# Two unrolled loops and a reordered state space layer in a six-layer kernel on one Trainium2 core

## The chip, the cores and the metric

The kernel runs on one core of one Trainium2 chip, in one launch. The metric is device time in microseconds (us). The core has five engines that run their own instruction queues and meet at semaphores: TensorE (PE, with PEld for its weight loads), VectorE (DVE), ScalarE (ACT), GpSimd (POOL) and SyncE (SP), which issues most of the DMA transfers.

## The reference

Six layers, each added to the residual `x` (128 sequences of 32 tokens, 256 channels), all behind a layer norm:

```python
x = x + L0_xattn(ln(x), ctx, ctx, mask)   # softmax cross-attention, 16 heads of 16, 257 context rows
x = x + L0_attn(ln(x))                    # state space layer, 16 states for each channel
x = x + L0_ffn(ln(x))                     # quantised feed-forward layer
x = x + L1_xattn(ln(x), ctx, ctx)         # the same attention with a sigmoid in place of the softmax
x = x + L1_attn(ln(x))                    # self-attention with a bias
x = x + L1_ffn(ln(x))                     # 8 experts, one for each token
```

The state space layer, cut to what matters:

```python
xc, z = split(x @ W_in.T)
xs = silu(conv3(xc))                       # over neighbouring tokens
dt = softplus(dt_param @ W_dt.T + b_dt) + 1e-5
s  = exp(-exp(A_log) * dt) * s + Bp * dt * xs          # scan over the 32 tokens
y  = (Cp @ W_C.T) * s.sum(-1) + D_param * xs
out = (y @ W_out.T) * silu(z)
```

## The kernel before

The residual stays in the on-chip memory (`all_xres`) through all layers. The layers run one after another, called x0 (softmax attention), m0 (state space), f0, x1 (sigmoid attention), a1 and e1; between two of them all engines meet. Matrix products are made from fp16 pairs (`...h` and `...l`, high and low part), three products for each.

**x0 and x1.** The unit of work is one sequence (128 of them). For each, PE makes the keys (`x_psK`) and values (`x_psV`) from the context, then the scores (`x_psS`: line 548 in x0, line 1190 in x1) and the attention sums; x0 also transposes the probabilities. ACT and DVE split each result into a high and a low part, POOL splits the context and spreads the queries. Four sequences make a group, which shares a tile of queries; eight sequences, two groups, make one body, so a layer is 16 bodies. Each engine has its own function `body(i)`, in which the order is written by hand: scores of sequence c, keys of c+2, transposes of c-1, values of c+1, attention of c-2 on PE, and so on. Where a body has an index that is a Python number, all its addresses and semaphore values are constants; where it is a loop's register, they are worked out at run time. The helper `run` (lines 251 to 255 in x0, 981 to 985 in x1) writes out body 0 and body 15 and puts the 14 between them in a hardware loop:

```python
def run(eng, body):
    body(0)
    with eng.Fori(1, LASTI) as i:
        body(i)
    body(LASTI)
```

In x0 the last context row is handled apart. `last_scores` (its products are recorded under line 432, as `x_psM<-x_kxh,x_qbdh`) runs once for each group, 24 products of two columns each, and takes its keys at an address that depends on the group.

**m0.** The unit is a tile of 256 tokens, 16 of them, four to a body; bodies 1 and 2 are in a hardware loop (line 1671). For a tile n, PE does `drive` (line 1852, products that fill `m_psBx`, four quarters), `state_sum` (line 1863, the sum over states, four pieces of eight), and for neighbouring tiles `xc` and `z` (input projections), `dbl` (the projection to dt, B and C parameters), `dt_c` (dt and C), `uT` (line 1839, a transpose of `m_u`), `xnT` and `out`. DVE scans each quarter (line 2077) and does the convolution, the low parts, `read_out` and `gate` (line 2091). ACT does the 32 exponentials of `decay` (line 1984), the logarithm `softplus_log` (line 1964), the two silu functions (lines 1930 and 1937) and high parts. POOL does `split_xs` (lines 1700 and 1702), `dt_u` (lines 1715 and 1718: dt, then u = dt times xs), `spread_b` (line 1725), `read_out` and `residual` (line 1743). `m_psBx` has one buffer: a quarter's drive waits for the scan of the quarter before it. The order on each engine is the order of the calls in `body`.

Of the kernel before, what the change touches and what calls it, by code (L numbers as in the profile page):

```python
# [180 lines left out]
def softmax_attention(nc, d, xres, con, norm):  # L181
# [4 lines left out]
    with ExitStack() as ctx:  # L186
# [62 lines left out]
        LASTI = NT // 2 - 1  # L249

        def run(eng, body):
            body(0)
            with eng.Fori(1, LASTI) as i:
                body(i)
            body(LASTI)

        def exists(i, c, off):
            return not isinstance(i, int) or 0 <= i * 8 + c + off < NB
# [664 lines left out]
def sigmoid_attention(nc, d, xres, con, norm):  # L923
# [4 lines left out]
    with ExitStack() as ctx:  # L928
# [50 lines left out]
        LASTI = NT // 2 - 1  # L979

        def run(eng, body):
            body(0)
            with eng.Fori(1, LASTI) as i:
                body(i)
            body(LASTI)

        def exists(i, c, off):
            return not isinstance(i, int) or 0 <= i * 8 + c + off < NB
# [627 lines left out]
def state_space(nc, d, xres, con, norm):  # L1616
# [7 lines left out]
    with ExitStack() as ctx:  # L1624
# [65 lines left out]
        @block.gpsimd  # L1690
        def _(pool):
            pool.memset(up[:], UP).then_inc(zeroed, 1)
            for h in range(C):
                pool.memset(A[h][:], 0.0).then_inc(zeroed, 1)

            def split_xs(i, c):
                n = i * U + c
                wait_apart(pool, xs_done, n + 1, pool_passed)
                wait_apart(pool, pb_mm, n, pool_passed)
                pool.tensor_scalar(xsp[0][:], xs[c % 2][:], 1.0, 1.0, ALU.mult, ALU.mult).then_inc(xs_hi, 1)  # L1700
                pool.wait_ge(xs_hi, n + 1)
                pool.tensor_tensor(xsp[1][:], xs[c % 2][:], xsp[0][:], ALU.subtract).then_inc(xs_lo, 1)

            def direct(i, c):
                n = i * U + c
                wait_apart(pool, y_done, n - 3, pool_passed)
                for h in range(C):
                    last = pool.tensor_scalar(dxs[c][:, h, :], xs[c % 2][:, h, :], d_par[:, h:h + 1], YS, ALU.mult, ALU.mult)
                last.then_inc(dxs_done, 1)

            def dt_u(i, c):
                n = i * U + c
                pool.wait_ge(soft_step, n * 4 + 4)
                wait(pool, a_done, (n - 1) * C)
                pool.tensor_tensor(dt[c % 2][:], sp_r[:], sp_a[:], ALU.add).then_inc(dt_done, 1)
                pool.wait_ge(dt_done, n + 1)
                wait(pool, u_mm, n - 1)
                pool.tensor_tensor(u[c % 2][:], dt[c % 2][:], xs[c % 2][:], ALU.mult).then_inc(u_done, 1)

            def spread_b(i, c):  # L1720
                n = i * U + c
                pool.wait_ge(pb_lo, n + 1)
                wait(pool, bx_mm, (n - 1) * 4)
                for k in range(2):
                    last = pool.tensor_tensor(Bd[c % 2][k][:], Bp[k][:].unsqueeze(2).to_broadcast([P, 2 * NS, T]),
                                              token[:].unsqueeze(1).to_broadcast([P, 2 * NS, T]), ALU.mult)
                last.then_inc(b_spread, 1)

            def read_out(i, c):
                n = i * U + c  # L1730
                pool.wait_ge(y_prod, n + 1)
                pool.tensor_tensor(y[:], y[:], dxs[c][:], ALU.add).then_inc(y_done, 1)
                wait_apart(pool, y_done, n + 1, pool_passed)
                wait_apart(pool, o_mm, n, pool_passed)
                pool.tensor_scalar(yp[0][:], y[:], 1.0, 1.0, ALU.mult, ALU.mult).then_inc(y_hi, 1)
                pool.wait_ge(y_hi, n + 1)
                pool.tensor_tensor(yp[1][:], y[:], yp[0][:], ALU.subtract).then_inc(y_lo, 1)

            def residual(i, c):
                n = i * U + c  # L1740
                pool.wait_ge(o_done, n + 1)
                row = xres[:, bass.ds(n * (2 * D), 2 * D)]
                pool.tensor_tensor(row, row, o[:], ALU.add).then_inc(x_done, 1)

            pool.wait_ge(const_in, 80)
            for c in range(2):
                split_xs(0, c)
                direct(0, c)
                if c == 0:
                    dt_u(0, 0)  # L1750
                    spread_b(0, 0)

            def body(i):
                for c in range(U):
                    if exists(i, c, 1):
                        spread_b(*at(i, c, 1))
                    if exists(i, c, -2):
                        residual(*at(i, c, -2))
                    if exists(i, c, 1):
                        dt_u(*at(i, c, 1))  # L1760
                    if exists(i, c, 2):
                        split_xs(*at(i, c, 2))
                    if exists(i, c, -1):
                        read_out(*at(i, c, -1))
                    if exists(i, c, 2):
                        direct(*at(i, c, 2))
            run(pool, body)
            residual(LASTI, U - 2)
            read_out(LASTI, U - 1)
            residual(LASTI, U - 1)  # L1770

        @block.tensor
        def _(pe):
# [111 lines left out]
            def body(i):  # L1885
                for c in range(U):
                    drive(i, c, 0)
                    if exists(i, c, 2):
                        xc(*at(i, c, 2))
                        z(*at(i, c, 2))  # L1890
                    if exists(i, c, -1):
                        state_sum(*at(i, c, -1), 1, 0)
                    drive(i, c, 1)
                    if exists(i, c, -1):
                        state_sum(*at(i, c, -1), 1, 1)
                    if exists(i, c, 1):
                        uT(*at(i, c, 1))
                    if exists(i, c, 3):
                        xnT(*at(i, c, 3))
                    drive(i, c, 2)  # L1900
                    state_sum(i, c, 0, 0)
                    if exists(i, c, -1):
                        out(*at(i, c, -1))
                    if exists(i, c, 2):
                        dbl(*at(i, c, 2))
                    drive(i, c, 3)
                    state_sum(i, c, 0, 1)
                    if exists(i, c, 2):
                        dt_c(*at(i, c, 2))
            run(pe, body)  # L1910
            state_sum(LASTI, U - 1, 1, 0)
            state_sum(LASTI, U - 1, 1, 1)
# [3 lines left out]
        def _(act):  # L1916
# [83 lines left out]

            def body(i):
                for c in range(U):
                    decay(i, c, 1, 0)
                    decay(i, c, 1, 1)
                    if exists(i, c, 1):
                        softplus_log(*at(i, c, 1))
                    if exists(i, c, 2):
                        silu_z(*at(i, c, 2))
                        silu_xs(*at(i, c, 2))
# [16 lines left out]
        def _(dve):  # L2026
# [75 lines left out]
            def body(i):  # L2102
                for c in range(U):
# [10 lines left out]
                    scan(i, c, 2)  # L2114
                    if exists(i, c, 2):
                        lo_pb(*at(i, c, 2))
                    scan(i, c, 3)
                    if exists(i, c, -1):
                        gate(*at(i, c, -1))
                    if exists(i, c, 4):  # L2120
                        ln(*at(i, c, 4))
            run(dve, body)
# [1076 lines left out]
```

## Time and profile before

| what | value |
|---|---|
| three timed runs | 3118.89, 3127.29, 3130.5 us (median 3127.29) |
| the profiled execution, its own time | 3123.87 us |
| its span in the trace | 3122.1 us |
| PE busy | 2561.8 us, 82% |
| DVE busy | 2130.9 us, 68% |
| ACT busy | 1878.5 us, 60% |
| POOL busy | 1542.9 us, 49% |
| mean granted TensorE clock | 0.913 of full speed |
| x0, from its first scores to its last | 56.6 to 940.5 us |
| m0, between the first and the last transposes and products of PE | 980 to 1475 us |
| x1, from its first scores to its last | 1660.6 to 2313.6 us |

How to read it: the engines work side by side, so their busy times do not add up to the span. A share over the whole span mixes six layers that have different limits; what a change in one layer is worth has to be read from that layer's own stretch. An idle time is given with what ended it: a tile of another engine, or "issue", where nothing that the profile shows was waited for.

### The profile page before, as it was taken

The page shows a single profiled execution, that of the slowest core. Times are in us where ns is not written, and L with a number is a line of the kernel's source. Part 1 is how long each engine was busy: PE and PEld are TensorE (multiplying, and loading weights), DVE is VectorE, ACT ScalarE, POOL GpSimd, SP SyncE. Part 2 cuts the span into 40 slices and gives each one's busy share as a digit, 9 for nine tenths or more (in the row PEclk, how much of TensorE's full clock was granted, in tenths as well). Part 3 has the DMA queues.
Part 4 walks back from the last instruction along what each step waited for, and adds up shares of the span by engine and source line. Part 5 has one row for each costly group of instructions (what it writes and reads, how often), then busy time and mean ns, then how long its engine had stood idle before and what let it go on. Part 6 is the DMA issues. An engine that isn't in the chain of part 4 may idle for free. (4 is left out here: it accounts for less than half of the span.)

```text
span 3122.1 us, 105389 instructions
## 1 busy us (share of the span) xinstructions
PE 2561.8 (82%) x38670; PEld 2034.0 (65%) x38671; DVE 2130.9 (68%) x4719; ACT 1878.5 (60%) x4388; POOL 1542.9 (49%) x1680
## 2 busy tenths in 40 slices
PE   3989889899893899996778989989967878509888
PEld 2867777677782577774446868768755666507666
DVE  5978878788794788886355757657665887643333
ACT  3867667677684788883346767667654665333333
POOL 4655656556562355552006656656635776052222
PEclk9999999999996899998898999999987998559999
DMA  4212212112110000000003212112100000641110
GB/s 144 67 59 59 64 51 64 58 51 64 57 30 14 1 1 1 0 1 14 16 14 91 66 50 62 59 52 61 59 18 3 2 2 2 206 159 34 33 34 27
DMA packets 120602, 144.45 MB, mean 46 GB/s; under 512 B 12912, under 2 KB 111632, under 8 KB 118064
## 3 DMA queue, kind: packets, MB, share of 16 engines
q1 hardware_dynamic: 115568, 124.40, 13.2%
q0 software_dynamic: 4672, 14.57, 1.3%
q8 instruction: 307, 5.03, 0.7%
q14 instruction: 55, 0.45, 0.0%
HBM read 123.71 MB, written 15.22 MB: 44 GB/s over the span
## 5 line engine op out<-in xcount | busy, mean ns | idle before, releaser
L1368 DVE SCALAR_TENSOR_TENSOR x_pTl<-x_psS,x_pTh 128x1024 f16<-128x1024 f32 x128 | 156.8, 1225 | 206.8 <-ACT x_pTh L1276 206.8
L2077 DVE TENSOR_TENSOR_SCAN m_s<-m_a,m_psBx 128x2048 f32<-128x2048 f32 x64 | 282.6, 4415 | 16.0 <-PE m_psBx L1852 15.6
L791 DVE CUSTOM_DVE_ANT_0 x_prob<-x_psS,x_masked,x_prob 128x256 f32<-128x256 f32 x512 | 216.6, 478 | 73.5 <-PE x_psS L548 71.7
L664 ACT ACTIVATE x_prob<-x_prob,x_low 128x257 f32<-128x257 f32 x512 | 253.5, 503 | 20.6 <-DVE x_low L791 20.6
L680 ACT ACTIVATE x_kh<-x_psK,x_bk 128x256 f16<-128x256 f32 x256 | 107.5, 471 | 238.9 <-PE x_psK L432 238.9
L1863 PE MATMUL m_psS<-m_s,all_ident 128*128 128x256 f32 x1024 | 237.3, 385 | 0.9 <-DVE m_s L2077 0.9
L1863 PEld LDWEIGHTS m_psS<-m_s,all_ident 128*128 128x128 f32 x1024 | 190.0, 190 | 46.3 <-issue 21.5
L1984 ACT ACTIVATE m_a<-m_dt,m_rate 128x248 f32<-128x248 f32 x512 | 205.6, 490 | 4.3 <-DVE m_s L2077 4.1
L2982 ACT ACTIVATE e1t_g<-e1t_psH,e1t_bias 128x128 f32<-128x128 f32 x312 | 89.2, 368 | 194.5 <-PE e1t_psH L2931 194.5
L1057 POOL TENSOR_TENSOR x_qbdh<-x_qh,all_mask4h 128x1024 f16<-128x1024 f16 x32 | 60.6, 1895 | 226.7 <-DVE x_ql L1349 226.7
L806 DVE SCALAR_TENSOR_TENSOR x_pTl<-x_psT,x_pTh 128x512 f16<-128x512 f32 x256 | 163.5, 679 | 4.9 <-ACT x_pTh L672 4.0
L1270 ACT ACTIVATE x_psS<-x_psS 128x1024 f32<-128x1024 f32 x128 | 129.0, 1008 | 59.7 <-PE x_psS L1190 57.3
L1049 POOL TENSOR_TENSOR x_ctxl<-x_ctx,x_ctxh 128x512 f16<-128x512 f32 x128 | 149.5, 1168 | 10.7
L337 POOL TENSOR_TENSOR x_ctxl<-x_ctx,x_ctxh 128x512 f16<-128x512 f32 x128 | 148.9, 1163 | 10.7
L432 PE MATMUL x_psK<-x_ctxh,x_wkh 128*128 128x256 f16 x512 | 148.3, 290 | 5.8 <-POOL x_ctxl L337 3.4
L2931 PE MATMUL e1t_psH<-e1t_xnh,e_wh 128*128 128x128 f16 x624 | 144.6, 232 | 9.0 <-issue 8.5
L1096 PE MATMUL x_psK<-x_ctxh,x_wkh 128*128 128x256 f16 x512 | 144.3, 282 | 4.5 <-POOL x_ctxl L1049 3.0
L432 PE MATMUL x_psK<-x_ctxh,x_wkl 128*128 128x256 f16 x512 | 147.8, 289 | 0.0
L432 PE MATMUL x_psK<-x_ctxl,x_wkh 128*128 128x256 f16 x512 | 147.8, 289 | 0.0
L1289 ACT ACTIVATE x_vh<-x_psV 128x512 f16<-128x512 f32 x128 | 76.4, 597 | 118.3 <-PE x_psV L1096 118.3
L672 ACT ACTIVATE x_pTh<-x_psT 128x512 f16<-128x512 f32 x256 | 138.9, 594 | 12.0 <-PE x_psT L558 9.2
L1096 PE MATMUL x_psK<-x_ctxl,x_wkh 128*128 128x256 f16 x512 | 143.3, 280 | 0.0
(558 smaller groups left out, 10542.0 us busy)
## 6 DMA issues: line engine op xcount, KB each, us to landing
x_ctx<-in_ctxT SPq DMA_DIRECT2D x64, 1024.0 KB, 5.7
x_mraw<-in_mask SPq DMA_DIRECT2D x128, 128.5 KB, 2.7
e1r_stage<-in_L_ffn_w SPq DMA_DIRECT2D x16, 1024.0 KB, 5.0
e_rows<-e1r_pad POOLq DMA_DIRECT2D x1, 5070.0 KB, 19.5
e1t_row<-e_rows SPq DMA_DIRECT2D x39, 130.0 KB, 2.1
all_xres<-in_x SPq DMA_DIRECT2D x1, 4096.0 KB, 14.8
x_vxr<-x_vx SPq DMA_DIRECT2D x128, 32.0 KB, 3.2
x_vxr<-x_vx SPq DMA_DIRECT2D x96, 8.0 KB, 2.0
```

Source lines behind the costliest of these rows:

```text
L337: pool.tensor_tensor(lo[:, j], src, hi[:, j], ALU.subtract).then_inc(ctx_split, 1)
L432: last = pe.matmul(out, a, b, start=m == 0, stop=m == len(prods) - 1)
L664: act.activation(prob[c % 4][:, h, :], prob[c % 4][:, h, :], ACT.Exp, bias=low[c % 4][:, h:h + 1], scale=-1.0, accum_out=sm[c % 2][:, h:h ...
L791: dve.tensor_tensor_reduce(prob[c % 4][:, h, 0:LAST], psS[:, to:to + LAST], masked[gp][:, j, 0:LAST], -SC, prob[c % 4][:, h, LAST:S2], ALU ...
L806: dve.scalar_tensor_tensor(pT[c % 2][1][:, kt, :], psT[:, kt * 512:(kt + 1) * 512], PS, pT[c % 2][0][:, kt, :], ALU.mult, ALU.subtract).th ...
L1049: pool.tensor_tensor(lo[:, j], src, hi[:, j], ALU.subtract).then_inc(ctx_split, 1)
L1096: last = pe.matmul(out, a, b, start=m == 0, stop=m == len(prods) - 1)
L1368: dve.scalar_tensor_tensor(pT[c % 4][1][:].rearrange("p r k n -> p (r k n)"), psS[c % 2][:], PS, pT[c % 4][0][:].rearrange("p r k n -> p ( ...
L1863: last = pe.matmul(psS[:, h * ST:(h + 1) * ST], con["ident"][:], S[h][:, :, m, :], start=m == 0, stop=m == NS - 1)
L1984: last = act.activation(A[h][:, :, m, 1:T], dt[c % 2][:, h, :].rearrange("p (b t) -> p b t", t=T)[:, :, 1:T], ACT.Exp, scale=rate[:, h, m: ...
L2077: dve.tensor_tensor_scan(rows(S), rows(A), psBx[:], 0.0, ALU.mult, ALU.add).then_inc(scan_done, 1)
L2931: last = pe.matmul(bank[:, k % 4 * P:(k % 4 + 1) * P], a, b, start=m == 0, stop=m == len(prods) - 1)
```

## The change

Three parts. In x0 and x1 `run` no longer makes a hardware loop: all 16 bodies are written out, on all five engines, with constants for every address and semaphore value. In m0, which keeps its loop, six calls change their place in the queues of POOL, PE, ACT and DVE. No operation is added or removed by hand.

```diff
@@ x0 (line 251) and, with the same text, x1 (line 981)
         def run(eng, body):
-            body(0)
-            with eng.Fori(1, LASTI) as i:
+            for i in range(LASTI + 1):
                 body(i)
-            body(LASTI)
@@ m0, POOL
                         spread_b(*at(i, c, 1))
+                        dt_u(*at(i, c, 1))
                     if exists(i, c, -2):
                         residual(*at(i, c, -2))
-                    if exists(i, c, 1):
-                        dt_u(*at(i, c, 1))
@@ m0, PE
                     state_sum(i, c, 0, 0)
+                    if exists(i, c, 2):
+                        dbl(*at(i, c, 2))
                     if exists(i, c, -1):
                         out(*at(i, c, -1))
-                    if exists(i, c, 2):
-                        dbl(*at(i, c, 2))
                     drive(i, c, 3)
-                    state_sum(i, c, 0, 1)
                     if exists(i, c, 2):
                         dt_c(*at(i, c, 2))
+                    state_sum(i, c, 0, 1)
@@ m0, ACT
+                    if exists(i, c, 1):
+                        softplus_log(*at(i, c, 1))
                     decay(i, c, 1, 0)
                     decay(i, c, 1, 1)
-                    if exists(i, c, 1):
-                        softplus_log(*at(i, c, 1))
@@ m0, DVE
-                    scan(i, c, 3)
                     if exists(i, c, -1):
                         gate(*at(i, c, -1))
+                    scan(i, c, 3)
```

The first place is PE in x0, in a body between the first and the last, where `last_scores` begins (`x_kxh` and `x_kxl` are the keys of the last context row, `x_qbdh` the queries). Before:

```order
L472 MATMUL x_psM<-all_ident,x_px 96x128
L476 ISA
L432 ISA
L432 MATMUL x_psM<-x_kxh,x_qbdh 128x2
L432 REGISTER_ALU
L432 MATMUL x_psM<-x_kxl,x_qbdh 128x2
L432 MATMUL x_psM<-x_kxh,x_qbdl 128x2
L432 ISA
```

Now (the file is five lines shorter here and there, so line numbers differ by two to five):

```order
L556 MATMUL x_psT<-all_ident,x_prob 128x128 x8
L470 MATMUL x_psM<-all_ident,x_px 96x128
L430 MATMUL x_psM<-x_kxh,x_qbdh 128x2
L430 MATMUL x_psM<-x_kxl,x_qbdh 128x2
L430 MATMUL x_psM<-x_kxh,x_qbdl 128x2
```

The register instructions between the products (`ISA` and `REGISTER_ALU`, one of each to every three products, eight times) are gone, and with them those at the waits of every body and the branch at its end.

The second place is PE in m0, the second half of a tile. Before (`m_psC<-m_xsh` is `dbl`, `m_psZ<-m_wouth` is `out`, `m_psC<-m_pbh` and `m_psU<-m_pbh` are `dt_c`, L1863 is `state_sum`):

```order
L1863 MATMUL m_psS<-m_s,all_ident 128x256 x8
L1777 MATMUL m_psZ<-m_wouth,m_yh 128x256
...
L1777 MATMUL m_psC<-m_xsh,m_wxh 96x256
...
L1852 MATMUL m_psBx<-m_bd1h,m_ut1l 128x512 x4
L1863 MATMUL m_psS<-m_s,all_ident 128x256 x8
L1777 MATMUL m_psC<-m_pbh,m_wdch 128x256
...
L1777 MATMUL m_psU<-m_pbh,m_wdch 128x256
```

Now:

```order
L1858 MATMUL m_psS<-m_s,all_ident 128x256 x8
L1772 MATMUL m_psC<-m_xsh,m_wxh 96x256
...
L1772 MATMUL m_psZ<-m_wouth,m_yh 128x256
...
L1847 MATMUL m_psBx<-m_bd1h,m_ut1l 128x512 x4
L1772 MATMUL m_psC<-m_pbh,m_wdch 128x256
...
L1772 MATMUL m_psU<-m_pbh,m_wdch 128x256
...
L1858 MATMUL m_psS<-m_s,all_ident 128x256 x8
```

`dbl` has moved ahead of `out`, and `dt_c` ahead of the last piece of the state sum.

The third place is ACT in m0, from the end of one tile to the middle of the next. Before:

```order
L1959 ACTIVATE m_sp_a<-m_sp_a 128x512
L1970 ACTIVATE m_c<-m_psU 128x512
L1984 ACTIVATE m_a<-m_dt,m_rate 128x8x31 x16
L1964 ACT_TABLE_LOAD
L1964 ACTIVATE m_sp_a<-m_sp_a,m_up 128x512
L1930 ACT_TABLE_LOAD
L1930 ACTIVATE m_zs<-m_psZ 128x512
```

Now:

```order
L1954 ACTIVATE m_sp_a<-m_sp_a 128x512
L1965 ACTIVATE m_c<-m_psU 128x512
L1959 ACT_TABLE_LOAD
L1959 ACTIVATE m_sp_a<-m_sp_a,m_up 128x512
L1979 ACT_TABLE_LOAD
L1979 ACTIVATE m_a<-m_dt,m_rate 128x8x31 x16
L1925 ACT_TABLE_LOAD
L1925 ACTIVATE m_zs<-m_psZ 128x512
```

The logarithm has moved ahead of the sixteen exponentials, and one more table load stands in each tile: the table is changed for the logarithm and changed back for the exponentials.

## Rows read from the trace of the kernel before

**Rows 1.** The page, part 1: busy us (share of the span) xinstructions

```profile
PE 2561.8 (82%) x38670; PEld 2034.0 (65%) x38671; DVE 2130.9 (68%) x4719; ACT 1878.5 (60%) x4388; POOL 1542.9 (49%) x1680
```

**Rows 2.** Windows, x0: stretch, length, busy PE PEld DVE ACT POOL, PEclk, DMA, GB/s

```profile
82.50:106.14 23.64, 23.09 (x458) 19.54 (x456) 21.74 (x69) 20.56 (x66) 14.53 (x23) 1.00 0.14 38
106.14:161.33 55.19, 48.92 (x911) 40.83 (x910) 48.05 (x148) 40.19 (x125) 39.45 (x61) 0.98 0.26 80
161.33:218.48 57.15, 50.74 (x908) 41.96 (x909) 46.10 (x142) 39.44 (x122) 33.77 (x50) 0.95 0.20 59
...
901.82:925.33 23.51, 22.89 (x456) 19.21 (x454) 21.07 (x67) 19.50 (x62) 16.16 (x25) 1.00 0.01 4
```

**Rows 3.** Waits in 106:902, PE and DVE: us in total, times, longest

```profile
PE x_psS L548 <- issue: 69.0, 13, 5.5
PE x_psS L548 <- DVE x_low L791: 10.5, 27, 0.5
...
DVE x_ql L765 <- ACT x_px L656: 28.2, 28, 1.3
...
DVE x_prob L791 <- issue: 0.3, 1, 0.3
```

**Rows 4.** Timeline of PE in x0: start, us, engine, line, operation, out<-in, [idle before]

```profile
97.46 0.17 PE L432 MATMUL x_psM<-x_kxh,x_qbdh 128*128 128x2 f16 x1
...
98.06 0.27 PE L432 MATMUL x_psV<-x_wvh,x_ctxh 128*128 128x256 f16 x1
...
106.14 0.28 PE L548 MATMUL x_psS<-x_kh,x_qbdh 64*128 64x256 f16 x2
...
146.01 0.17 PE L432 MATMUL x_psM<-x_kxh,x_qbdh 128*128 x1
...
147.95 0.27 PE L432 MATMUL x_psV<-x_wvh,x_ctxh 128*128 128x256 f16 x1
...
161.33 0.39 PE L548 MATMUL x_psS<-x_kh,x_qbdh 64*128 64x256 f16 x2 [5.36 <-issue]
...
901.82 0.28 PE L548 MATMUL x_psS<-x_kh,x_qbdh 64*128 64x256 f16 x2
```

**Rows 5.** Windows of x1, columns as in rows 2

```profile
1678.66:1697.82 19.16, 19.16 (x417) 15.65 (x417) 13.68 (x23) 14.42 (x23) 15.32 (x14) 1.00 0.33 97
...
1819.08:1865.80 46.72, 40.97 (x833) 32.89 (x834) 27.66 (x44) 28.95 (x46) 25.79 (x22) 0.90 0.18 54
```

**Rows 6.** Waits of the whole run for L1190, then the timeline of PE in x1

```profile
PE x_psS L1190 <- issue: 34.1, 6, 5.7
...
1697.82 0.23 PE L1190 MATMUL x_psS<-x_qbdh,x_kh 64*128 64x128 f16 x2
...
2282.23 0.23 PE L1190 MATMUL x_psS<-x_qbdh,x_kh 64*128 64x128 f16 x2
```

**Rows 7.** DMA queues in 56.6:161, 161.33:901.82, 1736.31:1810: packets, MB, share

```profile
q8 instruction: 15, 0.25, 1.0%
q14 instruction: 9, 0.07, 0.2%
...
q8 instruction: 116, 1.90, 1.1%
...
q14 instruction: 1, 0.01, 0.0%
```

**Rows 8.** m0: windows (columns as in rows 2), then the waits in 1060:1381

```profile
1060.00:1167.00 107.00, 99.98 (x747) 76.73 (x746) 93.72 (x73) 90.32 (x193) 54.59 (x48) 1.00 0.00 1
...
PE m_psU L1839 <- POOL m_u L1718: 18.2, 12, 1.6
```

**Rows 9.** Timeline of ACT and PE in one tile of m0

```profile
1172.68 1.28 ACT L1964 ACT_TABLE_LOAD   x1
1173.97 0.72 ACT L1964 ACTIVATE m_sp_a<-m_sp_a,m_up 128x512 f32<-128x512 f32 x1
...
1177.52 0.33 PE L1839 MATMUL m_psU<-all_ident,m_u 128*128 128x128 f32 x1 [1.57 <-POOL m_u L1718]
```

More of the change, by code:

```diff
@@ L981, in run @@
         def run(eng, body):
-            body(0)
-            with eng.Fori(1, LASTI) as i:
+            for i in range(LASTI + 1):
                 body(i)
-            body(LASTI)
         def exists(i, c, off):
```

## The prediction

> **What bounds the kernel now.** I read the page first: PE is the busiest engine, 82% of the span, DVE 68%, ACT 60% [rows 1]. That is a mean over six layers, so I went to the windows of the three layers that the change touches, then to the waits, then to the timeline where the waits said "issue".
>
> x0, between its bodies 1 and 14, is bound by PE with one hole per body. A body in the hardware loop lasts 57.15 us, in which PE is busy 50.74 and DVE 46.10 [rows 2]. Over the whole loop PE sat idle before the scores 13 times until "issue", 69.0 us in total, and 27 times on DVE for 10.5 us [rows 3]. The timeline shows where: 5.36 us before the first scores of body 2, at 161.33, but nothing at 106.14, where body 1 follows the written-out body 0, nor at 901.82, where body 15 follows the loop [rows 4]. Thirteen holes for 14 passes of the loop: they stand at the backward branch. The reader should also see the clock. It is 1.00 in the stretches without a hole and 0.95 in a body that begins after one [rows 2]; 1.00 is the 2.4 GHz level throughout, and 0.95 is a mean with a piece at 1.2 GHz in it, after PE had stood idle for 5.36 us.
>
> x1 shows the same, less often: 6 holes in 13 backward branches, 34.1 us [rows 6]. A body behind a hole has 40.97 us of PE work at a clock of 0.90, while a written-out half body lasts 19.16 us and is filled by PE to the last hundredth, at 1.00 [rows 5].
>
> m0 is nearly full on PE: 99.98 of 107.00 us (four tiles), DVE 93.72, ACT 90.32 [rows 8]. Most of PE's idle time there has one cause: the transpose of u waits for POOL, 18.2 us in 12 tiles, up to 1.6 us each [rows 8], and POOL waits for the logarithm on ACT, which stands behind sixteen exponentials.
>
> **The sum.** All of it is against the profiled execution, 3123.87 us for a span of 3122.1, which lies 3.4 us under the median of 3127.29.
>
> x0. The 14 bodies of the loop run from 106.14 to 901.82 [rows 4]: 795.7 us, or 56.83 each. The written-out code gives its own price in this trace. The second half of body 0, with every step of a full half body in it, lasts 23.64 us, and the first half of body 15, which lacks one layer norm and its transposes, 23.51 [rows 2]. I take 23.64: 28 halves make 661.9, so the gain is 133.8 us. Three things make it up. The holes are 69.0 [rows 3]. The register instructions between the 24 small products of `last_scores` stretch them from 97.46 to 98.06 (0.60 us) to 146.01 to 147.95 (1.94 us) [rows 4]: 1.34 us, 28 times, 37.5 us. What is left, 27 us, is about 2.1 us for each hole, the products that ran at the low clock behind it and the DVE work that came late. The ends of the gain: if the `last_scores` part does not come through, a body is body 1 without its hole, 55.19 - 5.36 = 49.83 [rows 2, 4], and the gain 98. If half bodies take 23.51, it is 137.
>
> Does DVE let PE run at 23.64? It is busy 46.10 in a body [rows 2], 23.05 in a half, and waits 2.0 us a body for ACT in `lo_q` (28.2 us in the whole loop, 28 times) [rows 3], which hangs on ACT's own queue and does not go with the holes. 23.05 + 1.0 makes 24.1 for a half, over 23.64. But in the half that I take the price from DVE did the same instructions. I keep 23.64 and give the difference to a rival.
>
> x1. The loop runs from 1697.82 to 2282.23 [rows 6], 584.4 us; 28 halves at 19.16 [rows 5] are 536.5. The gain is 47.9, of which 34.1 are holes [rows 6] and the rest the low clock behind them. The bounds are close, since seven bodies of the loop run at about 38.5 already: 42 to 49.
>
> Instruction fetch. The written-out bodies have to be read from memory as they run. For PE that is nothing new in x0: the instruction queue q8 brought 116 pages of 16 KB in 161.33 to 901.82, nine for each body, in the loop too, and 15 in the first two bodies [rows 7], where PE never waited for "issue" by 1 us. In x1 it is new, since the loop ran for whole bodies without a packet in q8 (1736.31 to 1810 shows q14 alone) [rows 7]; but the half body at 1678.66 ran from fresh pages and is full [rows 5]. The other engines' queue q14 brought 9 small pages in 56.6 to 161 and none in the loop [rows 7]. I cost all of it at nothing; the cover is that pages arrive ahead while the engine works on the last one, and DVE's longest wait for "issue" in x0 is 0.3 us [rows 3]. The Trainium skill, page "Runtime: NRT & Kernel Launch", section "Instruction fetch mechanics", says that prefetch runs straight ahead and that a taken branch whose target is outside a window of two pages has to fetch before it can go on. By that every backward branch of x1 would stall, 13 times, and the gain there would be about 13 x 7.6 = 99 us. The trace has 6 of 13 [rows 6], and loop and written-out half are both measured; they decide, and I stay at 47.9.
>
> m0. PE has 99.98 / 4 = 25.0 us of work in a tile of 26.75 [rows 8]. The reorder can give no more than the difference, 1.75. I expect it to give nearly that. The logarithm comes 16 exponentials sooner, so u is there before PE asks (1.57 us idle at 1177.52 [rows 9]). With `dbl` ahead of `out` and `dt_c` ahead of the last state sum, ACT gets both of its inputs earlier, and stands less between them and the next tile's softplus. What is paid: ACT gets one more table load in each tile, 1.28 us [rows 9], 90.32 / 4 + 1.28 = 23.9 us, still under 25.0, so PE hides it; `hi_u` now queues behind the silu functions, which the saved wait for u covers; `dt_c` may wait a few tenths for `lo_pb` on DVE; POOL's `residual` waits 1.3 us later behind `dt_u`, and nobody waits for it within the tile. Over 14 full tiles I take 14 x 1.75 = 24.5. The bounds: 0 if another wait takes the place, and a loss of 16 x 1.28 = 20 if ACT's load lands on the path. I take the gain because the three waits that the edits shorten are all on PE's side, and PE is the nearest to full. The Trainium skill, page "ScalarE: Activation LUTs", section "Table sets: the hidden batching unit", says that exponential and logarithm share one set, so that the moved logarithm would need no load at all. Here the logarithm has its own load of 1.28 us right ahead of it [rows 9]. By the page ACT would need 22.6 - 1.3 = 21.3 us a tile, before and after, and the sum would stay as it is, since PE ends the tile. The same page's section "What ACT_TABLE_LOAD costs" puts a switch at about 2.66 us with its drain; by that ACT would need 25.3 us a tile and m0 would gain about 4 us less.
>
> Sum: 133.8 + 47.9 + 24.5 = 206.2; 3123.9 - 206.2 = 2917.7, say **2918 us**. Other layers keep their code. Their loops may lose or gain a hole of some 5 us, since their pages lie elsewhere now.
>
> **Rivals.** *DVE becomes the bound of x0.* At 24.1 to 24.9 a half the gain is 121 down to 98 and the time 2930 to 2954. For it: the 2.0 us of waits a body [rows 3] and a busy share that is already 46.10 of 47.3. Against it: both written-out halves [rows 2].
>
> *m0 gives nothing or loses.* The table load and the silu functions behind the exponentials delay xs and u for the next tile; the time is 2942 with no gain, 2962 with a loss of 20. For it: ACT would be busy 95% of a 25 us tile. Against it: 1.1 us of slack.
>
> *The change doesn't do what it says.* The holes of x0 could belong to every ninth page and not to the branch, since there are nine pages to a body [rows 7]. Then written-out code keeps them, x1 stays as it is, and only `last_scores` and m0 gain: 3124 - 37.5 - 24.5 = 3062. Against it: 15 pages in the first two bodies without a hole, and 9 pages in x0 against none in x1 for much the same hole.
>
> *Slower than before.* The pages of DVE, ACT, POOL and SP, which the loops never reread, stall their engine. At 4.5 pages a body in x0 and about 2 in x1, that is some 90 pages; a stall of 5.4 us each, passed on to PE, costs 490 us, and the time is 3124 - 206 + 490 = 3408. It decides from 2.3 us a page. For it: in x0 DVE has half a microsecond of slack in a half body, so every stall would show. Against it: 0.3 us as the longest of DVE [rows 3] with 9 such pages read.
>
> **How the numbers follow.** Forecast 0.62; DVE-bound x0 0.18; m0 without gain 0.12; holes that stay 0.04; slower 0.03; no change at all, by some mixture, 0.01. The likeliest gives 2918. The low end is the upper bounds together (137 + 49 + 25 = 211) less the 5 us by which the timed runs lie under the profiled one: 2908, taken to 2902 for m0 edges. The high end takes in m0 without gain (2942) and nearly all of a DVE-bound x0 (2954), one at a time: 2950, which leaves out the losing m0, the holes that stay and the slower case, some 0.15 in all. A measurement of this kernel can tell about 0.5% (16 us) from no change. Faster by more: 0.96; within: 0.01; slower: 0.03.
>
> **What would show it.** In x0 no wait of PE for "issue" over 1 us before the scores, steps of 47.3 us from body to body, a clock of 1.00, and `last_scores` in 0.6 us each. In x1 steps of 38.3 us, PE full. In m0 tiles of about 25.0 us, no wait of PE for POOL's u, four table loads a tile. I am wrong if holes of 2 us or more appear anywhere in the written-out code, if DVE's wait for ACT in `lo_q` grows and PE waits for DVE's scores more than 0.5 us a half, or if m0's tile stays at 26.75.

## The result and the profile after

The changed kernel took 2898.18 us, median of 4 runs (2896.4 to 2903.61), against 3124.8 us for the kernel before on the same chip (4 runs, 3118.89 to 3130.5): a ratio of 0.9278 with a 95% interval of 0.9255 to 0.9301. The prediction was 2918 us with a range of 2902 to 2950. The direction and most of the size are right, but the time lies 4 us under the range: the prediction was wrong, and the last sections say by which step. The profiled execution took 2897.14 us, its span is 2895.3 us.

Part 1 of the page of the changed kernel, which answers to [rows 1]:

```profile
PE 2477.0 (86%) x38670; PEld 1973.2 (68%) x38671; DVE 2113.1 (73%) x4719; ACT 1896.3 (65%) x4402; POOL 1537.3 (53%) x1680
```

PE has the same 38670 products and is busy 84.8 us less, 66.3 of them in x0 and 13.7 in x1. I read this as the part of the gain that was low clock, or register instructions between products. ACT has 14 instructions more, the table loads of m0.

Windows of the changed kernel, columns as in [rows 2]: the second half of x0's body 0, bodies 1, 2, and the whole stretch of the former loop; then one body of x1 and its former loop:

```profile
82.00:105.58 23.58, 23.02 (x456) 19.49 (x454) 21.67 (x69) 20.50 (x66) 14.46 (x23) 1.00 0.15 37
105.58:152.60 47.02, 46.24 (x912) 38.89 (x910) 45.16 (x143) 39.48 (x123) 33.58 (x51) 1.00 0.26 71
152.60:199.60 47.00, 46.23 (x910) 38.89 (x908) 45.19 (x143) 39.51 (x124) 33.63 (x51) 1.00 0.25 71
105.58:764.18 658.60, 647.78 (x12716) 544.68 (x12714) 633.36 (x1989) 553.35 (x1709) 470.94 (x701) 1.00 0.25 71
1532.52:1570.84 38.32, 38.32 (x834) 31.33 (x834) 27.21 (x45) 28.85 (x46) 25.78 (x23) 1.00 0.21 64
1532.52:2069.92 537.40, 536.54 (x11649) 438.37 (x11649) 380.85 (x617) 403.89 (x644) 360.80 (x309) 1.00 0.21 63
```

A body of x0 lasts 47.0 us where it lasted 55 to 57 [rows 2], at a clock of 1.00 throughout; 14 bodies take 658.6 us in place of 795.7, a gain of 137.1 (forecast 133.8). DVE is busy 45.2 of the 47.0 us and never became the bound. x1's 14 bodies take 537.4 us in place of 584.4, a gain of 47.0 (forecast 47.9).

Waits of the changed kernel, in the whole run for PE and "issue", and in 105.58:764.18 for the two lines that the DVE rival spoke of. They answer to [rows 3] and [rows 6], where the scores of x0 waited 69.0 us and those of x1 34.1 us for "issue":

```profile
PE e1t_psH L2926 <- issue: 7.5, 26, 0.8
...
PE e1t_psY L2938 <- issue: 2.2, 11, 0.3
...
PE a_psS L2254 <- issue: 1.8, 1, 1.8
...
PE e1t_psX L2912 <- issue: 1.2, 3, 0.5
...
PE x_psV L1092 <- issue: 0.9, 1, 0.9
...
DVE x_ql L763 <- ACT x_px L654: 19.7, 28, 0.8
...
PE x_psS L546 <- DVE x_low L789: 5.3, 26, 0.3
```

The scores (now L546 and L1186) wait for "issue" nowhere. In all the written-out code of this kernel the longest such wait of PE is one of 0.9 us (`x_psV` in x1). DVE's wait in `lo_q` did not grow; it fell from 28.2 to 19.7 us.

`last_scores` in body 1 of x0, on the timeline of PE:

```profile
120.54 0.17 PE L430 MATMUL x_psM<-x_kxh,x_qbdh 128*128 128x2 f16 x1
120.57 0.16 PE L430 MATMUL x_psM<-x_kxl,x_qbdh 128*128 128x2 f16 x1
120.59 0.16 PE L430 MATMUL x_psM<-x_kxh,x_qbdl 128*128 128x2 f16 x1
120.62 0.16 PE L430 MATMUL x_psM<-x_kxh,x_qbdh 128*128 128x2 f16 x1
```

The products start every 25 ns, and 24 of them, from the first start to the last end, take 0.74 us, in the loop of the kernel before 1.95 to 2.10. Summed over the 32 groups that is 23.7 us in place of 59.4, so this part of the forecast (37.5 us) measured 35.7.

The diff of m0 moves five calls, not six as the section on the change counts them: `dt_u` on POOL, `dbl` and `dt_c` on PE, the logarithm on ACT and `gate` on DVE. m0 now: the window of one stretch (columns as in [rows 2]), the two waits that PE has in 903:1204 (twelve tiles), and the table loads of ACT in one tile; they answer to [rows 8, 9]:

```profile
1003.00:1103.00 100.00, 99.98 (x747) 76.28 (x745) 94.04 (x75) 95.82 (x198) 53.10 (x48) 1.00 0.00 1
...
PE m_psZ L1784 <- ACT m_zs L1925: 4.6, 1, 4.6
PE m_psC L1772 <- DVE m_bl L2055: 0.3, 1, 0.3
...
1045.41 1.28 ACT L1959 ACT_TABLE_LOAD   x1
1046.71 0.72 ACT L1959 ACTIVATE m_sp_a<-m_sp_a,m_up 128x512 f32<-128x512 f32 x1
1047.45 1.28 ACT L1979 ACT_TABLE_LOAD   x1
```

PE is full (99.98 of 100.00 us), a tile lasts 24.9 us (forecast 25.0, before 26.8), and the wait of the transpose for POOL's u (18.2 us in 12 tiles before) is gone. The one wait of 4.6 us stands at 906.65, in the last tile before the steps settle at 24.9. A table load takes 1.28 us and the next activation starts 0.02 us behind it, so the forecast's price for the added load was right: ACT is busy 24.0 us a tile, neither the 21.3 nor the 25.3 that the prediction worked out as the other cases. From its first instruction to its last, on any engine, m0 takes 481.5 us (822.6 to 1304.1) in place of 508.1 (960.1 to 1468.2): 26.6 gained, forecast 24.5.

These three parts make 210.7 us. The spans differ by 226.8. Nearly all of the missing 16 us lies in layers whose code is the same, measured like m0: 10.7 in e1t (the experts' products, behind everything else; 306.9 us before, 296.2 now), 2.6 in e1r (the router ahead of them), 2.5 in a1. In e1t the trace of before has these waits (stretch 2807:3115, lines of the kernel before):

```profile
PE e1t_psX L2917 <- issue: 9.0, 3, 4.6
PE e1t_psH L2931 <- issue: 8.5, 27, 0.7
```

The first line is two holes, 4.23 us at 2931.57 and 4.59 us at 2998.16, at the two backward branches of e1t's loop (line 2882); in the changed kernel the same wait has 1.2 us. The prediction gave them no weight. The question for the experiments was why they went, and whether the three large terms have the causes that I gave them.

### The profile page after: what moved, and what is told of

The parts are those of the page before. It is cut to its first block and busy times, and to the rows that moved or that the text cites. A ratio compares the mean times of both kernels' runs of the same rounds, so it can differ in the third digit from the quotient of the medians.

```text
span 2895.3 us, 99273 instructions
## 1 busy us (share of the span) xinstructions
PE 2477.0 (86%) x38670; PEld 1973.2 (68%) x38671; DVE 2113.1 (73%) x4719; ACT 1896.3 (65%) x4402; POOL 1537.3 (53%) x1680
## 5 line engine op out<-in xcount | busy, mean ns | idle before, releaser
L2072 DVE TENSOR_TENSOR_SCAN m_s<-m_a,m_psBx 128x2048 f32<-128x2048 f32 x64 | 282.8, 4418 | 21.6 <-PE m_psBx L1847 19.7
L1858 PEld LDWEIGHTS m_psS<-m_s,all_ident 128*128 128x128 f32 x1024 | 190.8, 191 | 43.3 <-issue 18.2
L1045 POOL TENSOR_TENSOR x_ctxl<-x_ctx,x_ctxh 128x512 f16<-128x512 f32 x128 | 149.5, 1168 | 10.7
L335 POOL TENSOR_TENSOR x_ctxl<-x_ctx,x_ctxh 128x512 f16<-128x512 f32 x128 | 149.2, 1166 | 10.7
L430 PE MATMUL x_psK<-x_ctxh,x_wkh 128*128 128x256 f16 x512 | 141.0, 275 | 4.6 <-POOL x_ctxl L335 3.4
L1092 PE MATMUL x_psK<-x_ctxh,x_wkh 128*128 128x256 f16 x512 | 141.0, 275 | 3.7 <-POOL x_ctxl L1045 3.0
L1092 PE MATMUL x_psV<-x_wvh,x_ctxh 128*128 128x256 f16 x512 | 140.8, 275 | 0.9 <-issue 0.9
L430 PE MATMUL x_psK<-x_ctxh,x_wkl 128*128 128x256 f16 x512 | 140.1, 274 | 0.0
L1092 PE MATMUL x_psK<-x_ctxh,x_wkl 128*128 128x256 f16 x512 | 140.1, 274 | 0.0
```

The lines of the kernel that those rows point to most:

```text
L335: pool.tensor_tensor(lo[:, j], src, hi[:, j], ALU.subtract).then_inc(ctx_split, 1)
L430: last = pe.matmul(out, a, b, start=m == 0, stop=m == len(prods) - 1)
L1045: pool.tensor_tensor(lo[:, j], src, hi[:, j], ALU.subtract).then_inc(ctx_split, 1)
L1092: last = pe.matmul(out, a, b, start=m == 0, stop=m == len(prods) - 1)
L1858: last = pe.matmul(psS[:, h * ST:(h + 1) * ST], con["ident"][:], S[h][:, :, m, :], start=m == 0, stop=m == NS - 1)
L2072: dve.tensor_tensor_scan(rows(S), rows(A), psBx[:], 0.0, ALU.mult, ALU.add).then_inc(scan_done, 1)
```

## The experiments

**The kernel before, once more.** No edit.

> The kernel before once more, unchanged, for a second trace of it. The question is the two holes of PE at the backward branches of e1t's loop (4.2 and 4.6 us in the first trace) and the six in x1 (5.6 to 5.7 us each). Theory 'place': whether a loop's pages are still held at its branch is fixed by where the code lies. Then this trace has the same holes at the same bodies: 13 in x0, 6 in x1 (34.1 us), 2 in e1t (9.0 us), and a time of 3117 to 3131 us. Rival 'chance': it differs from execution to execution. Then x1 has another number than 6 or holes at other bodies, e1t has 0 or 1, and the time moves by some 7 us for each hole.

3145.0 us. Waits of PE in this trace:

```profile
PE x_psS L548 <- issue: 68.9, 13, 5.5
...
PE x_psS L1190 <- issue: 45.7, 8, 6.1
...
PE e1t_psX L2917 <- issue: 9.6, 4, 4.9
```

Both theories hold somewhere. x0 has its 13 holes and e1t its two again, x1 has 8 holes in place of 6. Five traces have this x1 code at this place (the first, this one and three kernels below that change m0 alone), with 6, 8, 8, 6 and 6 holes in 13 branches: at that place the number is chance. The two holes more go with 18.2 us of the 21.1 by which this trace is longer than the first (x1 713.3 us in place of 695.1). The kernel before scatters from 3096 to 3150 us over all its runs, the changed kernel only from 2896 to 2904; chance in the number of holes is a likely cause, but the traces with 6 to 8 of them account for 15 us of that, not for 54.

**x0 alone, x1 alone, m0 alone.** Each takes one of the three parts of the change:

```diff
@@ x0 alone: run of x0; x1 alone: run of x1
-            body(0)
-            with eng.Fori(1, LASTI) as i:
+            for i in range(LASTI + 1):
                 body(i)
-            body(LASTI)
@@ m0 alone: the five moved calls, nothing else
```

> x0 written out, x1 and m0 as before. By my sum x0's loop part takes 661.9 us in place of 795.7 and the time is 3123.9 - 133.8 = 2990 us; what after's trace shows for x0 is 137.1, so 2987. x1 and e1t keep their loops, but their code now lies behind some 24,700 more PE instructions. By 'place' their holes may all come or go, and x1's number moves from 6 to another one; by 'chance' x1 has about 6 again. If DVE's wait in lo_q grew with PE's speed in x0, half bodies would take 24.1 to 24.9 us instead of 23.5.

> x1 written out, x0 and m0 as before. By my sum x1's loop part takes 536.5 us in place of 584.4: 3123.9 - 47.9 = 3076 us if the other layers keep their times. x0's loop lies where it lay, so its 13 holes stay (69 us). e1t's loop lies some 21,900 PE instructions later: by the theory that the last 15.8 us of the result come from where the later loops lie, its two holes (9.0 us) go or stay with that, and the time is 3076 if they stay and 3065 if they go.

> The six moved calls of m0 alone, all loops kept. By my sum m0 gains 14 x 1.75 = 24.5 us, after's trace has 26.6 from its first tile to its last: 3124 less 24.5 to 26.6 is 3097 to 3099 us. The number of PE instructions does not change, so every loop lies where it lay: by 'place' x1 keeps 6 holes and e1t 2, and a1, e1r and e1t keep their 332, 121 and 307 us; by 'chance' they differ. If m0's gain in the full kernel had come from anything in x0, its tiles would stay at 26.75 us here.

x0 alone: 3042.03 us against 3113.78, ratio 0.9777 (0.9752 to 0.9802), where I had expected 2987 to 2990. x0 itself did as forecast, with bodies of 47.0 us. But x1, whose code was not touched, became 54 us slower: its loop lasts 638.08 us in place of 584.4. Waits of PE for "issue" on the two lines, and the window of x1's loop, with x0 alone:

```profile
PE x_psS L1188 <- issue: 74.3, 13, 5.8
...
PE e1t_psX L2915 <- issue: 7.8, 2, 4.1
```

```profile
1561.64:2199.72 638.08, 562.63 (x11651) 454.19 (x11650) 386.13 (x617) 405.26 (x644) 360.89 (x309) 0.95 0.19 54
```

All 13 backward branches of x1 now have a hole. x1 alone: 3080.39 us, ratio 0.9898 (0.9872 to 0.9923); x1's 14 bodies take 538.3 us, 46 less, x0 keeps 13 holes (70.4 us) and e1t two (8.1 us). m0 alone: 3082.28 us (six runs, 3060.75 to 3116.27), ratio 0.9909 (0.9883 to 0.9936). Its trace is that of the longest run and has 8 holes in x1. It shows tiles of 24.9 us, so m0's gain owes nothing to the other parts, and e1t keeps its two holes (9.7 us). In the trace of x0 alone the span fell by 85.6 us, in that of x1 alone by 42.3, and m0's tiles alone give 27.8 (508.1 less 480.3): 155.7 together, where the whole change gives 226.8. The parts do not add up: of the missing 71 us, 54 are what x0 alone adds to x1, whose loop is gone in the whole change, and some 11 are e1t's, whose holes go in none of the three; the rest is made of small differences.

**The changed kernel again, and with its last loop shifted.** The second and third have products that nobody reads, ahead of e1t's first transposes, while PE waits 67.8 us there; they move only the code of e1t, loop included:

```diff
@@ e1t, PE, n = 32, 64 (96 in a later run)
+            for _ in range(n):
+                pe.transpose(psX[:, 0:P], con["ident"][:], con["ident"][:])
             transpose(0, 0)
```

> The changed kernel once more, unchanged, for a second trace. So far every trace with e1t's loop in the kernels before, x0 alone, x1 alone and m0 alone shows two holes of 3.7 to 5.1 us at e1t's backward branches, and only the changed kernel's none. If that is fixed by where its code lies: no hole in e1t again, e1t at 296 us, 2893 to 2904 us in all. If it was chance (as x1's number of holes, 6 in one trace of the kernel before and 8 in the next): about two holes, e1t at some 307 us, and 2904 to 2912 us.

> The changed kernel with 32 transposes of the identity, read by nobody, ahead of e1t's first transposes, in the 67 us in which PE waits for its normed tokens. They shift e1t's code by 64 instructions, a quarter of a 16 KB page if an instruction with its weight load takes two slots of 64 bytes. By 'place' this or the other shift brings the two holes back (e1t 307 us, total up by about 10 us); if the place within a page is of no account, e1t has none again (296 us, total within 5 us of the changed kernel's).

> The same with 64 such transposes, half a page by that count. By 'place' two holes in e1t in at least one of the two shifted kernels, so a time of about 2908 us; otherwise none, and 2893 to 2904 us.

2896.16, 2900.85 and 2905.43 us. No hole in e1t in any of the three: the loop's own wait for "issue" is 1.2, 1.2 and 1.3 us. The extra 4 and 9 us are not holes but the added transposes themselves: the 64 of them start at 2591.78, and the first one that is read at 2601.58. So the absence of holes in the changed kernel is no accident of one execution. Whether it is the place was still open: I had put down that the place theory wants two holes in one of these two kernels, and neither has any. The times at which q8's pages arrive told where to look. Counted from the transposes at the loop's second tile in its first pass, the next page comes after 3.8 to 5.1 us in the five traces that had two holes by then, and after 2.9, 2.8, 0.8 and 8.0 us in the four without (the expectations count from another point). A page lasts some 9.3 us there. 32 more transposes moved it by 2 us and a little more, so the next 32 should bring 8.0 down to between 5 and 6, beside the bad ones.

**Two forecasts of the place theory.** One shift that should bring the holes back in the changed kernel, and one that should take them away from the loops of the kernel before, x1's and e1t's alike. For this one 96 small products stand ahead of x1's first ones, where PE waits 24 us:

```diff
@@ kernel before, x1, PE
             def last_keys():
+                for _ in range(96):
+                    pe.matmul(psK[0:4, 0:4], con["mask4h"][:], con["mask4h"][:], start=True, stop=True)
                 pe.wait_ge(last_lo, 1)
```

> The changed kernel with 96 transposes read by nobody ahead of e1t, 32 more than the last one. It moves the first page of e1t's loop to about 0.5 us behind its start, where the kernels before, x0 alone, x1 alone and m0 alone have theirs (-0.4 to 2.5 us). 'Place in the page': two holes of 4 to 5 us at 2780 and 2845 us that the other three kernels of this family did not have, e1t some 10 us longer. Rival 'what was fetched before it': no hole.

> The kernel before with 96 products of four columns, read by nobody, ahead of x1's first products, in the 24 us in which PE waits for the last context row. The loops of x1 and e1t then lie 192 instructions of PE later, three quarters of a 16 KB page if each takes two slots of 64 bytes; x0's loop stays where it is. In the traces so far the pages of q8 arrive in the first pass of x1's loop at 3.6, 9.3, 14.4 ... us after its start (kernel before, 6 and 8 of 13 branches with a hole) and at 2.6, 8.5, 13.8 ... (x0 alone, 13 of 13); in e1t at 1.8 us (two holes) and at 7.2, 5.3, 3.5 us (the changed kernel and its two shifted forms: none). Theory 'place in the page': the three quarters move x1's first page to about 5 us and e1t's to about 5.5, each loop then touches one page less and stays held: no hole in x1 (x1's loop at 14 x 38.3 = 537 us, 47 less) and none in e1t (10 less), x0's 13 holes unchanged: about 3060 us with the kernel before at 3112. Rival 'what was fetched before it' (written-out code in front of the loop keeps its pages): nothing changes, 3100 to 3130 us, with 6 or more holes in x1.

The changed kernel with 96 transposes, 2922.61 us; waits of PE in 2595:2914, then the window of eight tiles without a hole and of eight with one:

```profile
PE e1t_psX L2912 <- issue: 9.0, 4, 4.3
...
2656.50:2718.20 61.70, 57.82 (x595) 44.20 (x594) 24.45 (x49) 21.20 (x80) 18.06 (x24) 1.00 0.12 35
2718.20:2784.60 66.40, 58.46 (x595) 45.72 (x593) 24.45 (x48) 21.20 (x80) 18.06 (x24) 0.95 0.12 34
```

The holes are back, two of them, from 32 transposes more than in a kernel that had none. The next page now comes after 5.2 us. What q8 brought in two passes of the loop shows the cause, first of this kernel (2718.16:2850.9), then of the changed kernel (2704.09:2825.9):

```profile
q8 instruction: 18, 0.29, 1.0%
```

```profile
q8 instruction: 1, 0.02, 0.1%
```

With holes, nine pages are fetched in every pass of a loop of 6.6 (a pass of 61.7 us at 9.3 us a page), so all of them again and some two more; without, PE runs from what it holds.

The kernel before with the shift of x1: 3069.34 us against 3126.51, ratio 0.9796 (0.9749 to 0.9843). Waits of PE, and the windows of x1's loop and of e1t:

```profile
PE x_psS L548 <- issue: 69.5, 13, 5.5
...
PE e1t_psX L2919 <- issue: 1.0, 3, 0.4
...
1704.20:2242.96 538.76, 537.68 (x11649) 438.41 (x11649) 385.31 (x617) 403.73 (x644) 360.47 (x309) 1.00 0.20 60
2769.30:3065.10 295.80, 279.74 (x2886) 217.29 (x2886) 119.05 (x234) 104.87 (x391) 87.04 (x116) 0.99 0.11 35
```

x1's loop, still a loop, has no hole: 538.8 us, 45.6 less than before, and only 1.4 more than written out. e1t takes 295.8 us in place of 306.9; its page comes 7.0 us behind the transposes that I count from, between the good 8.0 and the bad 5.2. What q8 brought in x1's 14 bodies, here (1704.20:2242.96), in the kernel before (1697.82:2282.23) and with x0 alone (1561.64:2199.72):

```profile
q8 instruction: 7, 0.11, 0.1%
```

```profile
q8 instruction: 61, 1.00, 0.8%
```

```profile
q8 instruction: 124, 2.03, 1.6%
```

That is 7 pages without a hole, 7 and 9 more for each of 6 holes, and 7 and 9 more for each of 13. 96 products that compute nothing make the kernel 2% faster. x0's loop was not moved and has its 13 holes. a1's loop moved too and has two short holes (4.8 us) where it had one (2.1 us). The rival, that it matters what was fetched ahead of the loop, falls: nothing was written out here.

**m0, one call at a time.** In the kernel before, the logarithm alone, then `dt_c` alone:

```diff
@@ ACT: the logarithm alone
+                    if exists(i, c, 1):
+                        softplus_log(*at(i, c, 1))
                     decay(i, c, 1, 0)
                     decay(i, c, 1, 1)
-                    if exists(i, c, 1):
-                        softplus_log(*at(i, c, 1))
@@ PE: dt_c alone
-                    state_sum(i, c, 0, 1)
                     if exists(i, c, 2):
                         dt_c(*at(i, c, 2))
+                    state_sum(i, c, 0, 1)
```

> Only one of the six moved calls, in the kernel before: the logarithm ahead of the sixteen exponentials, with its additional table load. My prediction took this for the main edit (u is there before PE asks: 1.5 of the 1.75 us a tile): tiles of 25.3 us in place of 26.8. Rival: with dt_c still behind the last state sum and dt_u behind residual, ACT's queue is the path, and the table load of 1.28 us lands on it: tiles of 27 us or more, slower than before.

> Only dt_c ahead of the last state sum, in the kernel before, no other of the six moves. If the logarithm's move is the main edit: tiles of 26.4 to 26.8 us, a few tenths gained at most. Rival: ACT waits for dt_c's product (1.6 and 1.4 us a tile for m_psC in the trace of before), and all else follows from it: then this move alone brings tiles near 25.1 us, almost all of the 1.9 us that the six bring together, with no additional table load.

The tiles last 28.2 us with the logarithm alone and 25.3 with `dt_c` alone (26.8 before, 24.9 with all six); the whole kernels 3143.04 and 3103.5 us. Waits in 1100:1310, eight tiles; first the logarithm alone:

```profile
ACT m_pbh L1944 <- PE m_psC L1777: 19.8, 8, 2.6
...
PE m_psZ L1789 <- ACT m_zs L1930: 14.1, 8, 1.8
...
ACT m_sp_r L1952 <- PE m_psC L1777: 11.0, 7, 1.6
```

then `dt_c` alone, where this is the largest wait of PE in the stretch:

```profile
PE m_psC L1777 <- DVE m_bl L2060: 3.2, 9, 0.4
```

What I took for the main edit makes m0 slower by 1.4 us a tile. It does what I said of it: PE waits for u no more in this stretch. But other waits take the place. In the same eight tiles of the kernel before, ACT waited 12.6 us for the product of `dt_c` (L1952) and 11.3 for that of `dbl` (L1944); now it is 11.0 and 19.8, the silu functions come later behind one more table load, and PE waits 14.1 us until they have emptied its buffer, and 7.1 us for POOL's low part of y. `dt_c` alone gives 1.5 of the 1.9 us, without a further load: ACT's wait for its product (12.6 us) is gone, and with it PE's wait for u (10.8 us in the same stretch of the kernel before). With the other four moved as well the tile is 0.4 us shorter still; which of them does it, the logarithm included, no run here tells.

**All loops written out.** Does the remedy reach further? m0, f0, a1 and e1t's tiles too (the router's loop in e1r and the norm's stay):

```diff
@@ run of m0, f0, a1 and e1t, on top of the change
-            body(0)
-            with eng.Fori(1, LASTI) as i:
+            for i in range(LASTI + 1):
                 body(i)
-            body(LASTI)
```

> The changed kernel with the loops of m0, f0, a1 and of e1t's tiles written out as well. If the backward branch is what lets PE stand, the one hole of 1.8 us in a1 and what is left in e1t (1.2 us) go, and e1t has none whatever its place: 2892 to 2896 us, no more than 5 us under the changed kernel, since no other loop has a hole. e1t's and a1's register instructions between products go too, a few tenths a tile: perhaps 5 us more. If instead code that is read once costs DVE, ACT or POOL something in these layers, m0's tiles grow over 24.9 us and the time lies over 2900.

2880.03 us, median of 6 runs (2879.14 to 2881.82), ratio to the kernel before 0.9255 (0.9217 to 0.9293), with the unedited changed kernel at 2896.16 in the same comparison. Windows of a1 and e1t with all written out, then of the changed kernel:

```profile
2121.20:2442.60 321.40, 241.05 (x4032) 197.96 (x4032) 246.60 (x510) 182.99 (x324) 214.37 (x162) 0.92 0.01 2
2588.30:2871.70 283.40, 276.26 (x2886) 216.20 (x2886) 118.84 (x234) 104.85 (x391) 87.00 (x116) 0.99 0.12 37
```

```profile
2117.20:2446.90 329.70, 248.84 (x4032) 204.31 (x4032) 247.30 (x511) 182.97 (x324) 214.71 (x162) 0.89 0.01 2
2591.80:2888.00 296.20, 279.72 (x2886) 216.43 (x2886) 119.09 (x234) 105.16 (x391) 87.12 (x116) 0.99 0.12 35
```

It is faster than both kernels, and the gain, 16 us, is more than the 5 to 10 I allowed. Holes were only 3 us of it. In e1t the gain comes in steps of about 0.5 us, one for each tile, ahead of the products `e1t_psH`: the waits of that line for "issue" fall from 7.5 us (26 times) to 2.6 (6 times). I read them as the register work on the loop's index ahead of each tile; that reading was not tried by itself. In a1 the clock rose from 0.89 to 0.92 and PE's work fell by 7.8 us; why, no run here tells. m0's tiles did not grow, so code read only once costs the other engines nothing there.

## Why the prediction was wrong, and where it was right

**The step that failed** is the last of the sum: "Other layers keep their code. Their loops may lose or gain a hole of some 5 us, since their pages lie elsewhere now." The sentence names the right mechanism and then costs it at zero, in the sum and in the range. The profiled execution gained 226.7 us, 20.5 more than the 206.2 of the sum. The three terms make up 4.5 of that. The layers behind x1 gave 15.8 us, 10.7 of them in e1t: two holes (8.8 us) and the low clock behind them. That these go by the place of the loop in its pages is shown from both sides: 32 transposes more bring them back in the changed kernel, 96 products take them out of the kernel before. With e1t's 10.7 us as one end of that term, the low end would have been 2891 and the range would have held 2898. The two holes stood in the waits of the trace of before, and the prediction reads only the stretches that the diff names. Its low end has a wrong reading besides: only the fastest of the three timed runs lies 5 us under the profiled one, their median 3.4 us above it. The remaining 5.1 us, in e1r and a1, are within what these layers differ by from trace to trace with the same code (a1 327.5 to 332.9 us over the traces that have its loop, e1r 118.4 to 121.9); I assign them to nothing.

**x0** measured 137.1, forecast 133.8: half bodies take 23.5 us, nearer to the 23.51 that I used as the bound than to 23.64. The split holds too: `last_scores` 35.7 of the forecast 37.5, no hole left, the clock at 1.00. The DVE rival falls: a busy share of 45.2 of 47.0 us is enough, as the written-out half had shown.

**x1** measured 47.0, forecast 47.9. The term was right for the profiled execution alone. It is a lottery of 6 to 8 holes at that place, each worth some 7.6 us with its low clock, so the term of another execution is up to 15 us larger.

**m0** measured 26.6, forecast 24.5: the size was reasoned, but that it was reached was in part luck. The limit that I worked out (PE's 25.0 us of work) was right and set the size; the chain that I told ("The logarithm comes 16 exponentials sooner, so u is there before PE asks") is true and brings nothing by itself: with the logarithm alone u is there and the tile lasts 28.2 us. `dt_c` was the edit that mattered. A sum that rests on "PE fills up" can be right while its story is not.

**Instruction fetch** at nothing in the written-out code was right: one wait of 0.9 us on PE (1.0 us with x1 alone), none above 0.5 us on DVE, ACT or POOL. The rivals of holes at every ninth page and of page stalls on the other engines both fall. What the prediction set against the first of them was misread: "none in x1 for much the same hole" goes by 1736.31 to 1810, and the first hole of that loop ends at 1819.08. Over the loop q8 brought 61 pages, nine with each hole, as in x0. The nine pages a body were the mark of the hole and not the size of the body.

Against the Trainium skill, page "Runtime: NRT & Kernel Launch", section "Instruction fetch mechanics", the runs stand on both sides. Its window of two pages at a taken branch does not agree with the traces: e1t's loop of some 6.6 pages ran for two passes on one packet of q8, and x1's for 14 bodies on 7. With x0 alone every branch of x1 did stall, and the loss of 99.3 us is what the prediction had worked out for that case; but this holds at one place of the loop and not at another. The same section of the Trainium skill gives PE 128 KiB of instruction memory, eight of the 16 KB pages; I had not weighed that sentence. It agrees with what was seen if a loop is held as long as the pages it touches, with one fetched ahead, fit in eight. Loops of 6.6 pages, e1t's and x1's (93 pages in 14 written-out bodies), touch seven or eight by where they begin. x0's takes 7.3 or more (102 pages in 14 written-out bodies), so it touches eight at least, and it had 13 holes in every trace that has its loop, though all of these have it at the same place. The size of the memory itself no run here shows, and that the limit lies between seven and eight pages is my reading, argued and not shown.

## What to carry to other kernels

A hardware loop of 6 to 7 pages of PE code can have a cost that depends on where it begins: 0, 6, 8 or 13 holes of 5.7 us for the same x1 code. So look for "issue" in the waits of every loop behind an edit, also where the edit did not touch it, and give such holes both signs in the range. Where writing a loop out is not wanted, shifting its start by less than a page is a test, and here a remedy, at the price of a few products in an idle stretch. And a reorder that comes as a packet of moves should be priced move by move: one of these five costs 1.4 us a tile alone, another brings 1.5.

## What was not expected of the hardware

- Whether a loop of PE is fetched again is fixed by its place in the page at some places (e1t: always two holes or never, in 13 traces; x1: 13 of 13 in one place, 0 in another, one trace each) and is chance at another (x1: 6 or 8 of 13).
- A hole of 5.7 us costs more than its length: x1's loop lost 99.3 us with 13 holes of 74.3 us in sum (638.1 against 538.8), so 1.9 us each came from the stretch behind, where the granted clock stood at 1.2 GHz for a while: its mean is 0.95 over the loop and 1.00 without holes.
- Written-out code of all five engines streams in with no wait over 0.9 us in the changed kernel, beside the layer's own transfers: in x0 102 pages by q8 and 50 by q14 in 658.6 us.
